# Biases off the matrix engine, quantised values transposed as 16-bit floats, and query and key rows restacked in 8 KB runs: a fused two-layer kernel on one core

## The chip, the cores and the metric

The kernel runs on one core of a Trainium2 chip. The metric is the device time of the whole program in microseconds, from the core's first to its last instruction as the runtime reports it; three runs of the kernel before gave 1095.13, 1095.16 and 1095.32 us (median 1095.16). A core has five engines with instruction streams of their own: PE (the 128x128 matrix engine), DVE (vector), ACT (scalar and activation), POOL (a second, slower vector engine) and SP, which here issues the DMA transfers. They meet only through semaphores.

## The reference

32 independent batches of 128 tokens with 256 features. With LN(v) = (v - mean) / sqrt(var + 1e-5), and mha() an attention of 16 heads of 16 features:

```
h  = LN(x)
a  = LN(h + mha(q=h, kv=h,   s_* weights and biases, mask S)) * ln1_g + ln1_b
c  = LN(a + mha(q=a, kv=ctx, c_* weights and biases, mask X)) * ln2_g + ln2_b
f  = relu(c @ ff_w1 + ff_b1) @ ff_w2 + ff_b2                 # 256 -> 1024 -> 256
x1 = x + tanh(g_x) * (LN(c + f) * ln3_g + ln3_b)
quant(v): s = 127 / max|v| per row, round(v * s) / s         # weights quantised to -1, 0, 1
g, u = quant(LN(x1)) @ w_gate.T, quant(LN(x1)) @ w_up.T      # 256 -> 1024
out  = x1 + tanh(g_f) * (quant(silu(g) * u) @ w_down.T)
```

## The kernel before

**Tiles.** A group is two batches (`G = 2`, `T = 256` tokens); there are 16 groups. A group passes through four stages: A (self attention), B (cross attention), C (the first feed-forward net) and E (the quantised one). The kernel is software-pipelined: iteration t works on stage A of group t-1, its preparation `Ap` of group t, B of group t-2, C of t-3 and E of t-4. So there are 20 iterations, the 5 first and 4 last written out and 11 in a hardware loop; iterations 4 to 15 have every stage at work.

**The order of the work** is a table, `SCHEDULE`, that all five engines walk in the same order, each doing its own part of a step. `("smax", k, quad)` and `("scores", k, half)` are the two score products of attention unit k (units 0 and 1 are the two batches of A, 2 and 3 those of B; 4 or -1 are the neighbours' in the next or last iteration); `values` the product with V; `R` turns its result back; `O` and `W` turn and project the output; `N` normalises; `M` turns the row maxima. `Ap` and `Bp` steps make the projections, `("in", s, t)` brings a stacked tensor back, `C F` and `C F2` are the two layers of the first net, `E GU`, `Q2` and `DN` gate/up, the second quantisation and the down projection. `BANK_OF` says which of four PSUM banks (lin_A, lin_B, lin_C, lin_E) a step writes. A step waits until its bank is read out and its inputs are there; an engine that waits holds up all that stands behind it.

**Precision by parts.** A 32-bit factor is split into an f16 high part and an f16 rest; `products` adds three products of parts.

**Biases.** They lie in two rows (high and rest) of `brows`. `bias` opens an accumulation with one matmul of `brows` against ones: two per projection of Q or K, two per `C F` step (line 595), one per `W` and per `C F2` (line 597).

**Quantised values.** ACT adds `MAGIC` = 1.5 * 2^23, which rounds to whole numbers in f32; PE turns the f32 tiles (`TQ` line 623, four blocks; `DN` line 760, four blocks for each of four steps), and ACT takes `MAGIC` off on the way out of PSUM (lines 859, 905).

**Restacking.** Scores need, for each head, its 16 rows of q (or k) high and rest stacked in the partitions. `parts_out` (line 472) writes both parts to DRAM as (2, 256 features, 256 tokens); `parts_in` (line 481) reads them back in four transfers of 16 partitions each, in runs of 512 bytes (one feature's 256 tokens). SP also copies the residuals `hres_A`, `hres_B` from `h` (lines 514, 507).

**Normalisation.** DVE takes the statistics (1067 to 1076), POOL the power -1/2 (1290), DVE applies it (1081), POOL multiplies by the gain (1308) and adds the bias (1316).

## Time and profile before

| | |
|---|---|
| median of 3 runs | 1095.16 us |
| profiled execution | 1097.78 us, span 1096.0 us |
| mean granted PE clock | 0.95 of full; 1.00 from 239 to 955 us |
| PE / DVE / ACT / POOL busy | 934.2 / 768.7 / 476.8 / 282.7 us |
| DMA | 85.02 MB in 136284 packets, 131631 of them under 2 KB |
| chain that ended last | PE 37%, DVE 24%, issue 14%, DMA 12%, POOL 5%, SP queue 5%, ACT 3% |

The profile is one execution. Busy time counts an engine's instructions; for PE, spans of consecutive matmuls overlap, so the distance between two starts is what a matmul costs the stream, and the printed mean is longer. "Idle before" is time in which an engine had no instruction running just before the rows of a group, with what ended it. The chain of waits follows the last instruction back through what released it each time.

### The profile page before, as it was taken

The page shows a single profiled execution, that of the slowest core. Times are in us where ns is not written, and L with a number is a line of the kernel's source. Part 1 is how long each engine was busy: PE and PEld are TensorE (multiplying, and loading weights), DVE is VectorE, ACT ScalarE, POOL GpSimd, SP SyncE. Part 2 cuts the span into 40 slices and gives each one's busy share as a digit, 9 for nine tenths or more (in the row PEclk, how much of TensorE's full clock was granted, in tenths as well). Part 3 has the DMA queues.
Part 4 walks back from the last instruction along what each step waited for, and adds up shares of the span by engine and source line. Part 5 has one row for each costly group of instructions (what it writes and reads, how often), then busy time and mean ns, then how long its engine had stood idle before and what let it go on. Part 6 is the DMA issues. An engine that isn't in the chain of part 4 may idle for free.

```text
span 1096.0 us, 26005 instructions
## 1 busy us (share of the span) xinstructions
PE 934.2 (85%) x8995; PEld 722.5 (66%) x8995; DVE 768.7 (70%) x1903; ACT 476.8 (44%) x769; POOL 282.7 (26%) x340
## 2 busy tenths in 40 slices
PE   1345869999999999999999999999999999877655
PEld 0224547768787777777777878687868687756442
DVE  7735555576878787877777787878787877664633
ACT  1113325254545455464545454545454545442422
POOL 7001112141323231323232323223141413140310
PEclk9959869999999999999999999999999999998885
DMA  6257273728191909081826464554637281514000
GB/s 166 89 85 133 63 86 74 93 63 104 44 133 40 135 29 144 29 137 37 127 47 111 53 101 72 84 75 88 83 80 91 65 99 49 60 49 39 21 10 10
DMA packets 136284, 85.02 MB, mean 78 GB/s; under 512 B 10632, under 2 KB 131631, under 8 KB 136240
## 3 DMA queue, kind: packets, MB, share of 16 engines
q1 hardware_dynamic: 136240, 84.43, 46.9%
q8 instruction: 28, 0.46, 0.2%
q14 instruction: 16, 0.13, 0.1%
HBM read 54.49 MB, written 20.98 MB: 69 GB/s over the span
## 4 chain that ended last, share of the span: by engine, by line
PE 37%; DVE 24%; issue 14%; DMA 12%; POOL 5%; SPq 5%; ACT 3%; DVEq 1%; POOLq 0%; ACTq 0%
DMA stk_BQ<-parts_BQ 9%; PE lin_C L747 5%; PE smax L663 4%; SPq L481 3%; PE lin_E L587 3%; PE lin_C L587 3%; POOL lrs L1290 3%; DVE nm_A L1145 2%; PE st L689 2%; DVE late L1081 2%; DVE lst L1067 2%; PE lin_E L736 2%; DVE am L1209 2%; PE lin_A L736 2%; PE lin_A L587 2%
## 5 line engine op out<-in xcount | busy, mean ns | idle before, releaser
L1290 POOL TENSOR_TENSOR lrs<-lve,neghalf 128x2 f32<-128x2 f32 (+1 forms) x112 | 71.0, 633 | 546.4 <-DVE lve L1076 546.3
L913 ACT ACTIVATE e<-st 128x1024 f32<-128x1024 f32 x128 | 130.8, 1022 | 58.8 <-PE st L689 57.9
L1145 DVE TENSOR_REDUCE nm_B<-smax 128x4 f32<-128x512 f32 x128 | 88.0, 687 | 55.0 <-PE smax L663 54.8
L1145 DVE TENSOR_REDUCE nm_A<-smax 128x4 f32<-128x512 f32 x128 | 87.9, 687 | 42.6 <-PE smax L663 39.3
L659 PE MATMUL smax<-mb,ident_big 128*128 128x512 f16 x128 | 52.6, 411 | 33.0 <-DVE nm_A L1145 23.0
L663 PE MATMUL smax<-stk_BK,stk_BQ 126*128 126x128 f16 x512 | 52.2, 226 | 19.3 <-DMA stk_BQ<-parts_BQ 14.5
L894 ACT ACTIVATE late<-late,magic_col,s 128x1024 f32<-128x1024 f32 x32 | 39.7, 1242 | 63.2 <-DVE s L1215 63.2
L919 ACT ACTIVATE av_sb<-av 128x512 f32<-128x512 f32 x64 | 37.9, 593 | 56.6 <-PE av L703 56.0
L663 PEld LDWEIGHTS smax<-stk_BK,stk_BQ 126*128 126x128 f16 x512 | 36.9, 100 | 33.3 <-DMA stk_BQ<-parts_BQ 11.5
L747 PE MATMUL lin_C<-w,late 128*128 128x256 f32 x256 | 57.9, 379 | 0.0
L747 PE MATMUL lin_A<-w,late 128*128 128x256 f32 x256 | 57.9, 379 | 0.0
L902 ACT ACTIVATE late<-lin_B,hcg 128x512 f32<-128x512 f32 x32 | 21.9, 686 | 81.8 <-PE lin_B L754 81.8
L663 PEld LDWEIGHTS smax<-stk_AK,stk_AQ 126*128 126x128 f16 x512 | 42.2, 103 | 17.5 <-issue 4.1
L663 PE MATMUL smax<-stk_AK,stk_AQ 126*128 126x128 f16 x512 | 53.2, 229 | 0.0
L684 PE MATMUL st<-mbT,ident_big 128*128 128x512 f16 x128 | 49.2, 384 | 3.6 <-ACT e L913 3.3
L747 PEld LDWEIGHTS lin_A<-w,late 128*128 128x128 f32 x256 | 47.4, 190 | 5.9
L747 PEld LDWEIGHTS lin_C<-w,late 128*128 128x128 f32 x256 | 47.4, 190 | 5.8
L689 PEld LDWEIGHTS st<-stk_AQ,stk_AK 128*128 128x128 f16 x512 | 39.7, 99 | 17.2 <-issue 0.6
L689 PE MATMUL st<-stk_AQ,stk_AK 128*128 128x128 f16 x512 | 50.0, 220 | 0.0
L659 PEld LDWEIGHTS smax<-mb,ident_big 128*128 128x128 f16 x128 | 12.6, 98 | 48.5 <-DVE nm_A L1145 33.0
L1296 POOL TENSOR_TENSOR qk_AQ<-qf_A,qk_AQ 128x512 f16<-128x512 f32 x16 | 18.5, 1157 | 97.9 <-ACT qk_AQ L867 97.9
L1081 DVE TENSOR_SCALAR late<-late,lmv,lrs 128x256 f32<-128x256 f32 x64 | 31.6, 535 | 15.3 <-POOL lrs L1290 15.2
(271 smaller groups left out, 2460.4 us busy)
## 6 DMA issues: line engine op xcount, KB each, us to landing
stk_AK<-parts_AK SPq DMA_DIRECT2D x64, 128.0 KB, 4.6
stk_AQ<-parts_AQ SPq DMA_DIRECT2D x64, 128.0 KB, 7.1
stk_BK<-parts_BK SPq DMA_DIRECT2D x64, 128.0 KB, 5.4
stk_BQ<-parts_BQ SPq DMA_DIRECT2D x64, 128.0 KB, 7.8
x_a<-in_x_dram SPq DMA_DIRECT2D x16, 256.0 KB, 2.9
cx<-in_ctx_dram SPq DMA_DIRECT2D x16, 256.0 KB, 2.8
parts_AK<-qk_AK SPq DMA_DIRECT2D x16, 256.0 KB, 6.4
parts_AQ<-qk_AQ SPq DMA_DIRECT2D x16, 256.0 KB, 4.5
```

What stands on the lines that cost most here:

```text
L587: mm = eng.matmul(dst, lhs(a, k), rhs(b, k), start=(start and at == 0), stop=(at == last))
L659: eng.matmul(smax[:, :], ident_big[:, :], mb[:, :].unsqueeze(1).to_broadcast([P, 4, P]), start=True, stop=True)
L663: mm = eng.matmul(smax[:, i * P:(i + 1) * P], stk[s, "Q"][0:XROW, h, tok], stk[s, "K"][0:XROW, h, tok], start=(s == "B"), stop=True, skip_ ...
L684: eng.matmul(st[:, k2 * 512:(k2 + 1) * 512], ident_big[:, :], mbT[:, :].unsqueeze(1).to_broadcast([P, 4, P]), start=True, stop=True)
L689: mm = eng.matmul(st[:, col:col + P], stk[s, "K"][:, h, tok], stk[s, "Q"][:, h, tok], start=(s == "B"), stop=True, skip_group_check=True)
L736: mm = eng.matmul(bank[:, 0:D], oT[s][:, c, :], wo[s][:, c, :], start=False, stop=(c == DC - 1))
L747: mm = eng.matmul(bank[:, 0:D], fT[:, c, k * P:(k + 1) * P], w2[:, c, :], start=False, stop=(c == FC - 1))
L894: eng.activation(q2m[:, :], z2[:, :], ACT.Identity, scale=s2[:, 0:1], bias=magic_col[:, 0:1]).then_inc(q2_ready, 1)
L913: eng.activation(e32[:, hf, :], st[:, :], ACT.Exp, scale=SCORE).then_inc(st_drained, 1)
L1081: i_ = eng.tensor_scalar(dst(k), src(k), lmv[n][:, k, 0:1], lrs[n][:, k:k + 1], ALU.subtract, ALU.mult)
L1145: eng.tensor_reduce(nm[s][:, 4 * part:4 * part + 4], smax[:, :].rearrange("p (h k) -> p h k", h=4), AX_X, ALU.max, negate=True).then_inc(s ...
L1290: eng.tensor_tensor(lrs[n][:, a:b], lve[n][:, a:b], neghalf[:, 0:b - a], ALU.pow).then_inc(ln_rstd[n], 1)
```

## The change

- The biases `s_bo`, `c_bo`, `ff_b2` are no longer matmuls in each `W` and `F2`. Three matmuls at the start spread them over the partitions, DVE makes `boA`, `lnbo_B` and `lnbo_C` (the latter two with `ln1_b`, `ln2_b` added), and POOL adds them into the residuals: `hres_A` and `hres_B` (128x512 each, in `residual`, in the place of SP's two copies) and a new `hres_C` (128x256 per batch, after `N`). `ff_b1` becomes the bias operand of the relu on ACT, which is one instruction per 256 columns in place of one per 512. The biases of Q and K stay on PE.
- ACT adds `MAGICQ` = MAGIC + 0x6600; the low 16 bits of the sum are then the f16 number 1536 + q. PE turns these halves (every second 16-bit element, f16 identity, f16 in PSUM), and ACT takes 1536 off.
- The columns of the Q and K weights are reordered within each half (by_dim, at the setup), so that 8 heads of one feature stand in 8 neighbouring partitions, and a partition's 2 x 256 columns are 1 KB. DRAM then holds, for one feature, 8 KB in one run. `parts_in` is two transfers of 32 partitions with 8 KB each. `parts_out` of a Q writes its high part twice, in a second transfer. `head_at` gives the head that stands in a slot.
- `SCHEDULE` and `BANK_OF` are new tables.

The core of the diff (the setup of reordered weights and bias rows, semaphore counts and the rest of the tables left out):

```diff
+LOW16 = 1536.0
+MAGICQ = MAGIC + 0x6600
...
+def head_at(slot):
+    return slot % DC * HB + slot // DC
...
-BIASES = [("s_bq", D), ("s_bk", D), ("c_bq", D), ("c_bk", D), ("ff_b1", F), ("s_bo", D), ("c_bo", D), ("ff_b2", D)]
+BIASES = [("s_bq", D), ("s_bk", D), ("c_bq", D), ("c_bk", D), ("s_bo", D), ("c_bo", D), ("ff_b2", D)]
...
-        part_dram = {(s, t): nc.dram_tensor(f"parts_{s}{t}", (2, D, T), F16).ap() for s in "AB" for t in "QK"}
+        part_dram = {(s, t): nc.dram_tensor(f"parts_{s}{t}", (3 if t == "Q" else 2, P, DC * T), F16).ap()
+                     for s in "AB" for t in "QK"}
...
-                eng.dma_start(part_dram[s, t].rearrange("q (c p) n -> p (q c) n", p=P),
-                              qk_parts[s, t][:, :, :]).then_inc(part_out[s, t], 16)
+                both = qk_parts[s, t][:, :, :].rearrange("p (q c) n -> p q (c n)", q=2)
+                eng.dma_start(part_dram[s, t][0:2].rearrange("q p x -> p q x"), both).then_inc(part_out[s, t], 16)
+                if t == "Q":
+                    eng.dma_start(part_dram[s, t][2], both[:, 0, :]).then_inc(part_out[s, t], 16)
 
             def parts_in(st_, s, t):
 
                 g = st_.g[s + "p"]
-                eng.wait_ge(part_out[s, t], g.at(16, 16))
-                for j in range(4):
-                    q = j // 2 if t == "Q" else j % 2
-                    eng.dma_start(stk[s, t][DH * j:DH * (j + 1), :, :],
-                                  part_dram[s, t][q].rearrange("(h d) n -> d h n", d=DH)).then_inc(stk_in[s, t], 16)
+                eng.wait_ge(part_out[s, t], g.at(PART_OUT[t], PART_OUT[t]))
+                for j in range(2):
+                    q = j if t == "Q" else 0
+                    rows = part_dram[s, t][q:q + 2].rearrange("q (d h) x -> (q d) (h x)", d=DH)
+                    eng.dma_start(stk[s, t][2 * DH * j:2 * DH * (j + 1), :, :].rearrange("p h n -> p (h n)"),
+                                  rows).then_inc(stk_in[s, t], 16)
...
-                        wait(eng, *st_.unit_read("W", -1))
-                        eng.dma_start(hres["B"][:, :, :], hin["B"][:, :, :]).then_inc(hres_in["B"], 16)
...
-                        wait(eng, *st_.unit_read("W", 1))
-                        eng.dma_start(hres["A"][:, :, :], hin["A"][:, :, :]).then_inc(hres_in["A"], 16)
...
-                            mm = eng.transpose(bank[:, at:at + P], q1m[:, b, c * P:(c + 1) * P], ident[:, :])
+                            low = q1m[:, b, c * P:(c + 1) * P].bitcast(F16).rearrange("p (n two) -> p n two", two=2)
+                            mm = eng.transpose(bank[:, :].bitcast(F16)[:, at:at + P], low[:, :, 0], ident16[:, :])
...
-                        bias(dst, "ff_b1", f * P, P, T)
...
-                for i in range(8):
-                    h = 8 * hf + i
+                for i in (0, 2, 4, 6, 1, 3, 5, 7):
+                    h = head_at(8 * hf + i)
...
-                bias(bank[:, 0:D], "s_bo" if s == "A" else "c_bo", 0, D, 0)
...
-                    bias(bank[:, 0:D], "ff_b2", 0, D, 0)
...
+            for i, name in enumerate(("s_bo", "c_bo", "ff_b2")):
+                col = BCOL[name]
+                eng.matmul(st[:, i * D:(i + 1) * D], ones16[:, 0:P], brows[:, col:col + D], start=True,
+                           stop=True).then_inc(u_pe, 1)
             first = first_steps()
-            for st_ in first[0:3]:
+            iteration(first[0])
+            eng.wait_ge(u_bo, 3)
...
-                    f, func = 2 * name[1], ACT.Relu
-                    eng.activation(fT[:, f:f + 2, :].rearrange("p f n -> p (f n)"), src, func).then_inc(drain, 1)
+                    for j in range(2):
+                        f = 2 * name[1] + j
+                        a_ = eng.activation(fT[:, f, :], bank[:, j * T:(j + 1) * T], ACT.Relu, bias=b1w[:, f:f + 1])
+                    a_.then_inc(drain, 1)
...
-                    eng.wait_ge(ln_bias[2], g.at(G, k + 1))
-                    eng.scalar_tensor_tensor(res["C"][:, k, :], bank[:, 0:D], 1.0 / (WS * WS), hin["C"][:, k, :],
+                    eng.wait_ge(hres_in["C"], g.at(G, k + 1))
+                    eng.scalar_tensor_tensor(res["C"][:, k, :], bank[:, 0:D], 1.0 / (WS * WS), hres["C"][:, k, :],
                                              ALU.mult, ALU.add).then_inc(drain, 1)
...
+            n_bo = [0]
+            eng.wait_ge(u_pe, 8)
+            setup(eng.tensor_scalar(boA[:, :], st[:, 0:D], 1.0 / WS, None, ALU.mult), u_bo, n_bo)
+            setup(eng.scalar_tensor_tensor(lnbo["B"][:, :], st[:, D:2 * D], 1.0 / WS, lnb[1][:, :], ALU.mult, ALU.add), u_bo, n_bo)
+            setup(eng.scalar_tensor_tensor(lnbo["C"][:, :], st[:, 2 * D:3 * D], 1.0 / (WS * WS), lnb[2][:, :], ALU.mult,
+                                           ALU.add), u_bo, n_bo)
...
+                    if s == "B":
+                        eng.tensor_tensor(hres["C"][:, b, :], tg[s][:, b, :], lnbo["C"][:, :], ALU.add).then_inc(hres_in["C"], 1)
+            def residual(st_, s):
+                if st_.reg is None and st_.t == 0:
+                    eng.wait_ge(u_bo, 3)
+                if s == "A":
+                    eng.wait_ge(ln_out[0], st_.g["Ap"].at(1, 1))
+                    wait(eng, *st_.unit_read("W", 1))
+                    src, add = hin["A"], boA
+                else:
+                    eng.wait_ge(ln_gain[1], st_.g["Bp"].at(G, G))
+                    wait(eng, *st_.unit_read("W", -1))
+                    src, add = tg["A"], lnbo["B"]
+                eng.tensor_tensor(hres[s][:, :, :], src[:, :, :], add[:, :].unsqueeze(1).to_broadcast([P, G, D]),
+                                  ALU.add).then_inc(hres_in[s], 1)
...
+                    elif step == ("Ap", "V"):
+                        residual(st_, "A")
+                    elif step == ("Bp", "Q"):
+                        residual(st_, "B")
```

PE around the first net's four `F` steps and the second layer. Before, rows of one iteration (`L595` and `L597` are biases, `L587` the products of the first layer, `L747` of the second, `L663` smax of B, `L736` the output projection):

```order
L663 MATMUL smax<-stk_BK,stk_BQ 128x128 x4
L595 MATMUL lin_C<-ones,brows 128x256
L587 MATMUL lin_C<-hT_C,w_0 128x256 x2
L587 MATMUL lin_C<-hT_C,w_1 128x256
L587 MATMUL lin_C<-hT_C,w_0 128x256 x2
L587 MATMUL lin_C<-hT_C,w_1 128x256
L595 MATMUL lin_C<-ones,brows 128x256
```

Now, the same step (`L610` the products, `L683` smax of B) and what follows it:

```order
L683 MATMUL smax<-stk_BK,stk_BQ 128x128 x4
L772 MATMUL lin_A<-wuT,q1T 128x512 x2
L755 MATMUL lin_E<-wo_A,oT_A 128x256 x2
L772 MATMUL lin_B<-wgT,q1T 128x512 x2
L693 MATMUL lin_C<-ident,nm_B 32x128
L683 MATMUL smax<-stk_BK,stk_BQ 128x128 x4
L772 MATMUL lin_E<-wuT,q1T 128x512 x2
L765 MATMUL lin_A<-w,late 128x256 x8
```

No `brows` row stands ahead of the projections (L755) or of the second layer (L765), and the gate and up products (L772) of the second batch now lie before the second layer instead of after it.

SP from the query rows of B to the read-back of A. Before:

```order
L472 DMA parts_BQ<-qk_BQ 128x4x256
L507 DMA hres_B<-h 128x512
L481 DMA stk_BK<-parts_BK 16x16x256 x4
L481 DMA stk_BQ<-parts_BQ 16x16x256 x4
L472 DMA parts_AK<-qk_AK 128x4x256
L519 DMA x_c<-in_x_dram 128x2x256
L472 DMA parts_AQ<-qk_AQ 128x4x256
```

Now:

```order
L499 DMA parts_BQ<-qk_BQ 128x2x512
L501 DMA parts_BQ<-qk_BQ 128x512
L510 DMA stk_BK<-parts_BK 32x4096 x2
L510 DMA stk_BQ<-parts_BQ 32x4096 x2
L542 DMA x_c<-in_x_dram 128x2x256
L499 DMA parts_AK<-qk_AK 128x2x512
L499 DMA parts_AQ<-qk_AQ 128x2x512
```

The residual copy is gone, a second write of the query rows has come, and eight reads are four.

DVE around the second layer of the first net and the second quantisation (`L1184`, now `L1226`, is the residual sum after `F2`; `L1209`, now `L1251`, the maximum of the second quantisation; `L1200` and `L1205`, now `L1242` and `L1247`, the gate and up products). Before:

```order
L1184 SCALAR_TENSOR_TENSOR late<-lin_C,h 128x256
L1142 REGISTER_ALU
L1145 TENSOR_REDUCE nm_B<-smax 128x4
L1199 REGISTER_ALU
L1200 SCALAR_TENSOR_TENSOR late<-late,lin_B 128x512
L1202 REGISTER_ALU
L1203 REGISTER_ALU
L1205 TENSOR_TENSOR late<-late,lin_E 128x512
L1209 TENSOR_REDUCE am<-late 128x1
```

Now:

```order
L1247 TENSOR_TENSOR late<-late,lin_E 128x512
L1224 REGISTER_ALU
L1226 SCALAR_TENSOR_TENSOR late<-lin_A,hres_C 128x256
L1184 REGISTER_ALU
L1187 TENSOR_REDUCE nm_B<-smax 128x4
L78 REGISTER_ALU
L1123 TENSOR_SCALAR nrm_A<-res_A,lmv,lrs 128x256
L1251 TENSOR_REDUCE am<-late 128x1
```

The gate and up products have moved ahead of the first `F2`; the maximum still follows it.

## Rows read from the trace of the kernel before

**Rows 1.** The page, busy us (share of the span) xinstructions

```profile
PE 934.2 (85%) x8995; PEld 722.5 (66%) x8995; DVE 768.7 (70%) x1903; ACT 476.8 (44%) x769; POOL 282.7 (26%) x340
```

**Rows 2.** Windows: start:end, length, busy us (x) of PE, PEld, DVE, ACT, POOL; clock, DMA

```profile
0.00:186.00 186.00, 101.12 (x873) 71.77 (x877) 110.53 (x202) 48.31 (x73) 38.77 (x44) 0.83 0.48 96
...
515.00:570.00 55.00, 53.10 (x531) 42.47 (x532) 43.30 (x110) 27.30 (x44) 15.84 (x19) 1.00 0.55 87
```

**Rows 3.** Timeline of ACT, line 859, first and thirteenth of 16: start, us

```profile
239.58 0.60 ACT L859 ACTIVATE q1T<-lin_A 128x512 bf16<-128x512 f32 x1
...
926.77 0.60 ACT L859 ACTIVATE q1T<-lin_A 128x512 bf16<-128x512 f32 x1
```

**Rows 4.** Waits of PE, 460 to 1010 us: total us, times, longest

```profile
PE smax L659 <- DVE nm_A L1145: 11.1, 17, 1.0
PE smax L663 <- DMA stk_BQ<-parts_BQ: 8.9, 7, 3.9
```

**Rows 5.** Timeline of PE: start, us of the group

```profile
522.26 0.39 PE L663 MATMUL smax<-stk_AK,stk_AQ 126*128 126x128 f16 x4
522.49 0.60 PE L617 MATMUL lin_C<-ident,h 128*128 128x128 f32 x4
522.93 0.38 PE L684 MATMUL st<-mbT,ident_big 128*128 128x512 f16 x1
...
551.00 0.28 PE L597 MATMUL lin_C<-brows,ones 128*128 128x256 f16 x1
551.11 3.62 PE L747 MATMUL lin_C<-w,late 128*128 128x256 f32 x16
554.56 0.39 PE L663 MATMUL smax<-stk_BK,stk_BQ 126*128 126x128 f16 x4
```

**Rows 6.** Groups by shape, ACT: busy us, mean ns, idle before

```profile
L852 ACT ACTIVATE late<-late,magic_col,s 128x256 f32<-128x256 f32 x32 | 17.5, 594 | 49.1 <-DVE kap L1110 49.1
...
L928 ACT ACTIVATE oT_B<-lin_E 128x256 f32<-128x256 f32 x32 | 12.4, 388 | 31.2 <-PE lin_E L724 31.2
...
L883 ACT ACTIVATE late<-lin_C 128x512 f32<-128x512 f32 x16 | 9.6, 597 | 18.5 <-PE lin_C L587 18.5
```

**Rows 7.** The page, DMA issues: KB each, us to landing

```profile
stk_BQ<-parts_BQ SPq DMA_DIRECT2D x64, 128.0 KB, 7.8
x_a<-in_x_dram SPq DMA_DIRECT2D x16, 256.0 KB, 2.9
...
parts_AQ<-qk_AQ SPq DMA_DIRECT2D x16, 256.0 KB, 4.5
```

**Rows 8.** Chain of waits, steady and first iterations: start, us, what

```profile
101.88 7.99 DMA stk_AQ<-parts_AQ
...
190.99 7.86 DMA stk_BQ<-parts_BQ
...
533.85 8.78 DMA stk_BQ<-parts_BQ
```

**Rows 9.** Timeline of POOL: start, us

```profile
509.70 1.27 POOL L1328 TENSOR_TENSOR late<-late,lnb 128x512 f32<-128x512 f32 x1
511.13 1.31 POOL L1333 TENSOR_TENSOR late<-late,x_c 128x512 f32<-128x512 f32 x1 [0.16 <-POOL late L1328]
...
515.78 0.73 POOL L1316 TENSOR_TENSOR h<-tg_B,lnb 128x256 f32<-128x256 f32 x1 [0.16 <-POOL tg_B L1308]
```

**Rows 10.** Timeline of DVE, same columns

```profile
491.68 0.17 DVE L1154 SCALAR_TENSOR_TENSOR nm_B<-nm_B 128x16 f16<-128x16 f32 x1
...
500.26 1.22 DVE L1209 TENSOR_REDUCE am<-late 128x1 f32<-128x1024 f32 x1
...
511.34 1.13 DVE L1154 SCALAR_TENSOR_TENSOR nm_A<-nm_A 128x16 f16<-128x16 f32 x1
```

**Rows 11.** Timelines at an iteration's start, DVE, then PE

```profile
515.00 0.69 DVE L1145 TENSOR_REDUCE nm_A<-smax 128x4 f32<-128x512 f32 x1 [0.18 <-issue]
...
515.75 0.39 PE L659 MATMUL smax<-mb,ident_big 128*128 128x512 f16 x1 [0.92 <-DVE nm_A L1145]
```

More of the change, by code:

```diff
@@ L589, in products, with bias @@
                 return mm
-            def bias(dst, name, start_col, width, tokens):
+            def bias(dst, name, start_col, tokens):
                 col = BCOL[name] + start_col
-                if tokens:
-                    eng.matmul(dst, brows[:, col:col + P], ones16[:, 0:tokens], start=True, stop=False)
-                else:
-                    eng.matmul(dst, ones16[:, 0:P], brows[:, col:col + width], start=True, stop=False)
+                eng.matmul(dst, brows[:, col:col + P], ones16[:, 0:tokens], start=True, stop=False)
             def prep(st_, s, name):
@@ L858, in prep @@
                     eng.wait_ge(fill, after)
-                    eng.activation(q1T[:, :, :].rearrange("p c n -> p (c n)"), bank[:, :], ACT.Copy,
-                                   bias=-MAGIC).then_inc(drain, 1)
+                    eng.activation(q1T[:, :, :].rearrange("p c n -> p (c n)"), bank[:, :].bitcast(F16)[:, 0:DC * T], ACT.Copy,
+                                   bias=-LOW16).then_inc(drain, 1)
                     return
@@ L893, in beside @@
                         wait(eng, *st_.full("E", ("DN", k - 1, 1)))
[L894 removed]
+                    eng.activation(q2m[:, :], z2[:, :], ACT.Identity, scale=s2[:, 0:1], bias=magicq[:, 0:1]).then_inc(q2_ready, 1)
                     return
@@ L1005, in low_part @@
                 eng.wait_ge(u_hi, sum(1 for m in range(n + 1) if m not in WHOLE))
+                if n in BY_DIM:
+                    for x_ in range(DC * DC):
+                        i_ = eng.scalar_tensor_tensor(by_dim(lo)[:, x_, :, :], heads_of(raw[n])[:, x_, :, :], WS,
+                                                      by_dim(hi)[:, x_, :, :], ALU.mult, ALU.subtract)
+                    setup(i_, u_lo, n_lo)
+                    return
                 setup(eng.scalar_tensor_tensor(lo[:, :, :].rearrange("p c n -> p (c n)"), raw[n], WS,
@@ L1244, in _ @@
             first = first_steps()
-            for st_ in first[0:3]:
-                iteration(st_)
-            for st_ in first[3:]:
+            iteration(first[0])
+            n_bo = [0]
[4 more added lines that the diff above has]
+                                           ALU.add), u_bo, n_bo)
+            for st_ in first[1:]:
                 iteration(st_)
@@ L1311, in unit_step @@
                         wait(eng, *st_.full("B", "T"))
-                        wait(eng, hres_in["B"], g.back(1).at(16, 16))
                     else:
```

80 lines of the change are left out of this document (56 added, 24 removed), and 38 rows, old and new, of tables (BANK_OF, SCHEDULE).

## The prediction

> **What bounds the kernel now.** I read four views, from coarse to fine. The page first: PE is busy 85% of the span, DVE 70%, ACT 44%, POOL 26% [rows 1]. Then the windows: of 55 us in mid-kernel PE is busy 53.1 and DVE 43.3, of the first 186 us PE only 101; its granted clock is 1.00 of full (2.4 GHz) in the one and 0.83 on the mean in the other [rows 2]. So the kernel has two regimes: a steady one in which PE is nearly full, and two ends that live on latency. The steady one is measured by one instruction that comes once an iteration: the turned quantised values leave PSUM at 239.58 us and, twelve iterations on, at 926.77 [rows 3]. That is (926.77 - 239.58) / 12 = 57.27 us an iteration, 687 us of the 1096. What stops PE there: in 550 us (9.6 iterations) it waits 11.1 us for DVE's row maxima and 8.9 us for the stacked query rows of stage B [rows 4], 1.16 and 0.93 us an iteration; the other waits are small. The chain of waits tells the less comfortable half: it does not stay on PE. In one steady iteration it goes through a transfer of 8.78 us (query rows of B), and in the ramp through transfers of 7.99 and 7.86 us [rows 8]. PE is full, but DVE, POOL and DMA chains end only just in time beside it.
>
> **Biases off PE.** A bias matmul costs the stream the distance between its start and the next: 551.11 - 551.00 = 0.11 us [rows 5]. In an iteration 8 go from `F`, 4 from `W`, 2 from `F2`: 14 x 0.11 = 1.54 us.
>
> **Transposes in f16.** Four f32 blocks take 522.93 - 522.49 = 0.44 us; four f16 products of 128 columns take 522.49 - 522.26 = 0.23 us [rows 5]. Twenty blocks an iteration (4 `TQ`, 16 `DN`) change from one to the other: 5 x 0.21 = 1.05 us. The trace has no f16 transpose with a stride of two in its weights. The bounds are 0 (it costs as the f32 one) and 1.05; I take 1.05, since the nearest row by type and columns is the f16 one.
>
> The Trainium skill's "TensorE: Matmul & The Clock Gate", the part on sustained rate, gives about 81 ns per matmul of 128 columns. By it four blocks would cost 0.32 us, and the term would be 0.58 us instead of 1.05. The trace has 0.23 us for four, 57 ns each, so I go by the trace.
>
> PE sheds 1.54 + 1.05 = 2.59 us of 57.27 an iteration.
>
> **Restacking.** A tensor of 512 KB now comes by four transfers of 128 KB, landing 7.8 us after issue by the median, in runs of 512 bytes; x comes with 256 KB in runs of 1 KB in 2.9 us [rows 7]. The changed read is two such 256 KB transfers in runs of 8 KB. Its bounds are 2.9 us and the old 7.8; I take 4.5, nearer to the row of x, since two follow each other. Against it: a query tensor is written with 384 KB instead of 256, where 256 KB landed in 4.5 us [rows 7], which I take as 1 us more, and SP waits for both. Net some 2.5 us sooner, and SP has four transfers fewer ahead of the B query read and no residual copy. In the steady state this can give no more than the wait it ends, 0.93 us; I take 0.9. The new order puts four `smax` of B between `F` steps, about the same distance behind `Bp Q`, so the wait should not come back.
>
> **Residuals on POOL.** POOL gets two sums of 128x512, 1.27 us each, and two of 128x256, 0.73 us each [rows 9]: 2.54 + 1.46 = 4.0 us an iteration on an engine busy 15.8 of 55 [rows 2]. The `residual` of B stands ahead of the power for unit -1: POOL waits for DVE's sum of `W -1`, then holds 1.27 us, beside which DVE takes the statistics of that unit. That makes DVE's `N -1` late by less than 1.27 us, I take 0.4; behind it are `GU` and a scores step, so PE is hidden. The `residual` of A stands behind the power of `W 2` and ahead of `N 2`. Its 1.27 us delay the gain and bias of B's last unit and then the power of E's norm; I count 1 us of room there. I cost all this at 0.1 us.
>
> A more direct cost is seen in the trace: the 16-column rest of the maxima takes DVE 0.17 us at 491.68, and 1.13 us at 511.34, ending at 512.47, as POOL's sum of 511.13 + 1.31 = 512.44 ends [rows 9, 10]. So a POOL sum can hold a small DVE step for its whole length. Four more sums an iteration are four more chances. If each hit costs 0.5 us and half of them hit, DVE loses 1 us, of which PE sees some 0.3.
>
> The Trainium skill's "SBUF — State Buffer", section "Who interferes with whom", says that these two share one port pair as an exclusive lock, and the loser blocks until the other is through; by that rule, the trace agrees.
>
> **Relu.** One instruction of 128x512 at 0.597 us becomes two of 128x256, each between 0.388 (no operand for the bias) and 0.594 us (with one) [rows 6]. Eight an iteration: 3.1 to 4.8 us against 2.4, on an engine that is half idle. The `F` rows come 0.2 to 0.6 us later; only the last before `F2` matters, and gate and projection steps lie between them now. Cost: 0.
>
> **The order.** At an iteration's start DVE is behind: the first maxima are taken at 515.00, and PE's second `smax` waits 0.92 us for them [rows 11]. The table changes nothing in the first ten steps, so a stall of this kind stays, and as PE comes sooner by what it sheds in the tail it may grow by 0.2 us. What gets better is the stretch from `F2 0` on: the gate and up products of the second batch are done before it, so that the quantisation's maximum, 1.22 us on DVE [rows 10], no longer waits for them. I take 0.3 us of gain, between -1 and +1.5.
>
> **The sum.** An iteration: 2.59 (PE) + 0.9 (transfer) - 0.1 (residuals) - 0.3 (held DVE steps) - 0.2 (start) + 0.3 (order) = 3.2 us, times 12 = 38 us. The ends hold four groups' worth of the same PE work, 4 x 2.59 = 10.4 us, in a regime where PE is busy half the time: 5 us. In the ramp four reads lie open at about 8 us (two of them shown [rows 8]); at 2.5 us less each they give 10, of which I keep 7, since other waits are next. The setup gains by shorter bias rows and loses by weights split in four pieces, three more matmuls and a wait: 0. Sum 38 + 5 + 7 = 50 us. The profiled execution, 1097.8 us, would become 1048; it lies 2.6 us over the median, which becomes 1095.2 - 50 = 1045 us.
>
> **Rivals.**
> 1. *The chain holds, not PE.* The chain of waits leaves PE for DVE, POOL and the transfer in much of a steady iteration. What PE sheds there turns into waiting, above all for the maxima. For it: 1.16 us of that wait are there already. Against it: DVE has 11.7 us free of 55. If half of PE's gain goes, an iteration gives 1.3 + 0.5 = 1.8, so 22 us, and with 8 from the ends 30: 1065 us.
> 2. *The strided weights cost as much as before.* Then 1.05 x 16 = 17 us are missing: 1045 + 17 = 1062 us.
> 3. *The order is better than I can see.* PE is idle 1.9 of 55 us [rows 2], 2.0 an iteration, of which my sum takes away 0.6 net. If all goes, that is 12 x 1.4 = 17 us more: 1028 us. For it: PE is the fullest engine by 10 us. Against it: the waits for maxima at the iteration's start, where the order is the old one.
> 4. *Slower: POOL holds DVE.* Each of the four new sums blocks a DVE step in full, and the late norms stop PE: 4.0 us more waiting against 2.59 less work, 1.4 us an iteration, 17 us in twelve, with nothing from the ends: 1112 us. It decides from 2.6 us of new waits an iteration on; 2.0 us are idle now. For it speaks the step held for 1.13 us [rows 10], against it that DVE is idle 11.7 of 55 us and that few such steps are there.
> 5. *The reads are no faster.* 32 runs of 8 KB could serve the 16 engines worse than 256 of 512 bytes; then 0.9 x 12 + 7 = 18 us are missing: 1063 us.
>
> **Numbers.** Forecast 0.5; rivals 1, 2 and 5 together 0.27; rival 3 0.12; rival 4 0.06; near zero, gains and waits in balance, 0.05. A measurement of this kernel can tell about 0.2%, 2.2 us. Faster by more 0.89, within 0.04, slower 0.07. The range runs from rival 3 to a little past rival 1: 1026 to 1070 us.
>
> **What the profile would show.** PE work: no `brows` rows but for Q and K, four turned blocks in 0.23 us, an iteration of 54 us between two `q1T`. Reads: a `stk_BQ` landing at 4 to 5 us, no wait of PE for it, and prologue transfers of that length in the chain. POOL: 20 us busy in 55, and few DVE steps of 16 columns beyond 0.2 us. I am wrong in mechanism if the iteration is over 55.5 us, if the waits for `nm_A` or `nm_B` exceed 2 us an iteration, or if `lin` rows of `TQ` keep a distance of 0.11 us.

## The result, and the profile after

The changed kernel takes 1057.64 us, the median of four runs (1056.64 to 1058.59), against 1095.14 for the kernel before on the same chip: a ratio of 0.966, with a 95% interval of 0.9643 to 0.9676. Forecast were 1045 us and a range of 1026 to 1070. So the sign and the range hold, and 12.6 us of the forecast gain did not come. The profiled execution of after has a span of 1054.9 us, 41.1 less than that of before; the working below goes by this pair.

The page of after, its busy line (us, share of the span, instructions), then its DMA packets and one line of the DMA issues (KB each, us to landing):

```profile
PE 891.9 (85%) x8730; PEld 687.2 (65%) x8774; DVE 780.6 (74%) x1921; ACT 501.2 (48%) x833; POOL 343.3 (33%) x405
...
DMA packets 57450, 80.81 MB, mean 77 GB/s; under 512 B 9623, under 2 KB 52798, under 8 KB 53310
...
stk_BQ<-parts_BQ SPq DMA_DIRECT2D x32, 256.0 KB, 5.0
```

Against [rows 1] PE is busy 42.3 us less in the whole span and POOL 60.6 us more. Some 7 of the 42.3 us are no saving: this trace lacks 44 matmul records (8730 beside 8774 weight loads). The trace of x2 below, with the same matmuls and all 8774 records, has PE busy 899.2 us. Against [rows 7] the query rows of B land after 5.0 us instead of 7.8, and packets fell from 136284 to 57450.

The windows of [rows 2], now (start:end, length, busy us and count of PE, PEld, DVE, ACT, POOL; granted clock, DMA share, GB/s):

```profile
0.00:186.00 186.00, 99.47 (x857) 70.18 (x858) 122.90 (x219) 54.36 (x73) 45.30 (x50) 0.86 0.32 93
515.00:570.00 55.00, 52.56 (x542) 41.48 (x544) 44.31 (x116) 29.94 (x51) 19.97 (x25) 1.00 0.32 80
```

The second row says that the steady state is what it was: PE nearly full at its full clock. POOL's 19.97 us is the 20 that was forecast. The first shows DVE 12 us busier in the ramp, most of it by the setup, below: with another setup (x2) DVE is busy 771.6 us in the whole span instead of 780.6.

The instruction that came once an iteration at 239.58 and 926.77 [rows 3] is now on line 887. Its first and thirteenth start in after are 235.00 and 896.90 us, so an iteration takes (896.90 - 235.00) / 12 = 55.16 us instead of 57.27. The 41.1 us are then 25.3 from twelve iterations, 4.6 before the first of them and 11.2 after the thirteenth start (158.0 us against 169.2).

The waits of PE in after, 294 to 900 us, 11.0 iterations (total us, times, longest):

```profile
PE smax L679 <- DVE nm_A L1187: 20.1, 22, 1.4
PE lin_E L693 <- DVE nm_A L1196: 2.8, 11, 0.3
PE lin_A L772 <- issue: 1.8, 11, 0.2
PE smax L683 <- DMA stk_BQ<-parts_BQ: 0.9, 3, 0.3
```

and in before over the same window, 10.6 iterations:

```profile
PE smax L659 <- DVE nm_A L1145: 13.3, 20, 1.0
PE smax L663 <- DMA stk_BQ<-parts_BQ: 4.2, 6, 1.3
PE smax L659 <- issue: 0.5, 2, 0.3
PE lin_A L595 <- DVE late L1200: 0.2, 1, 0.2
```

That makes 18.2 / 10.58 = 1.72 us an iteration before and 25.6 / 10.99 = 2.33 after. What is left of an iteration, PE's own stream with its small gaps, is 55.55 and 52.83. One row of after is no wait: `lin_A L772 <- issue` stands where the record of a matmul is missing (three of the sixteen matmuls of `L772` in an iteration; x2, with all its records, has no such row). Without it the waits are 2.16 and the rest is 52.99. So PE shed 2.6 to 2.7 us, as forecast (2.59), and the waits grew by 0.45 to 0.61 where the forecast had them shrink by 0.6. That difference is the size of the whole miss of the steady state. It does not say yet what the order of the steps has to do with it; x6 does. The transfer's wait is gone (0.40 to 0.08), the wait for stage A's maxima grew from 1.26 to 1.83, and a new one (line 693) is 0.25.

**Where the new wait comes from.** DVE in after, at the start of an iteration (start, us):

```profile
553.67 1.27 DVE L1123 TENSOR_SCALAR nrm_B<-res_B,lmv,lrs 128x256 f32<-128x256 f32 x1 [0.73 <-POOL lrs L1338]
554.87 0.68 DVE L1187 TENSOR_REDUCE nm_A<-smax 128x4 f32<-128x512 f32 x1
```

POOL in after, the same stretch:

```profile
553.02 0.55 POOL L1338 TENSOR_TENSOR lrs<-lve,neghalf 128x1 f32<-128x1 f32 x1 [1.63 <-DVE lve L1118]
553.53 1.26 POOL L1384 TENSOR_TENSOR hres_A<-h,boA 128x512 f32<-128x512 f32 x1
```

PE in after:

```profile
555.61 0.39 PE L679 MATMUL smax<-mb,ident_big 128*128 128x512 f16 x1 [1.43 <-DVE nm_A L1187]
```

Read them together. POOL delivers the power and at once starts the new residual sum of A, which ends at 554.79. DVE's normalising step starts beside it and is through only at 554.94, after 1.27 us. Behind that step on DVE stands the maximum for which PE waits: 1.43 us, where it was 0.92 [rows 11]. Over the whole run the step takes 793 ns on the mean (groups of DVE in after, busy us and mean ns):

```profile
L1123 DVE TENSOR_SCALAR nrm_B<-res_B,lmv,lrs 128x256 f32<-128x256 f32 x32 | 25.4, 793 | 19.0 <-POOL lrs L1338 19.0
...
L1194 DVE TENSOR_SCALAR nm_A<-nm_A 128x16 f16<-128x16 f32 x32 | 19.0, 595 | 3.2
...
L1196 DVE SCALAR_TENSOR_TENSOR nm_A<-nm_A 128x16 f16<-128x16 f32 x32 | 5.6, 175 | 1.1
```

In before these are:

```profile
L1081 DVE TENSOR_SCALAR nrm_B<-res_B,lmv,lrs 128x256 f32<-128x256 f32 x32 | 13.1, 409 | 11.8 <-POOL lrs L1290 11.7
...
L1152 DVE TENSOR_SCALAR nm_A<-nm_A 128x16 f16<-128x16 f32 x32 | 17.1, 536 | 3.2
L1154 DVE SCALAR_TENSOR_TENSOR nm_A<-nm_A 128x16 f16<-128x16 f32 x32 | 13.2, 413 | 1.1
```

The held step of [rows 10] (the rest of the maxima, 1.13 us) is gone, 413 to 175 ns, and a step that PE waits for is held instead. The two have different causes. Groups of DVE in x7, the kernel before with nothing but the new order:

```profile
L1081 DVE TENSOR_SCALAR nrm_B<-res_B,lmv,lrs 128x256 f32<-128x256 f32 x32 | 13.2, 413 | 13.1 <-POOL lrs L1290 12.4
...
L1154 DVE SCALAR_TENSOR_TENSOR nm_A<-nm_A 128x16 f16<-128x16 f32 x32 | 5.6, 175 | 1.1
```

The order alone frees the small step; the new sum holds `nrm_B`. The Trainium skill ("SBUF — State Buffer", "Who interferes with whom") has the two engines block each other for a whole instruction on a shared port pair. The trace agrees in the main: the held step ends 0.15 us after the sum. But it takes 0.41 us when alone, so one that could do nothing before the sum's end should end 0.41 us after it; these rows don't settle why it ends sooner.

**The setup.** DVE in after:

```profile
25.45 2.43 DVE L1038 SCALAR_TENSOR_TENSOR w_AQ<-late,w_AQ 128x128 f16<-128x128 f32 x4
...
40.08 2.42 DVE L1061 CAST e<-late 1x1024 f16<-1x1024 f32 x1
```

The same piece in before:

```profile
25.85 0.69 DVE L1006 SCALAR_TENSOR_TENSOR w_AQ<-late,w_AQ 128x512 f16<-128x512 f32 x1
```

The reordered weights are written as f16 with 16 bytes from one element to the next: 2.43 us for four quarters instead of 0.69 for the whole. The bias rows are cast in the same manner, and leave for their place late. SP in after:

```profile
48.80 0.65 SPq L483 DMA_DIRECT2D brows<-e  x1
```

and in before:

```profile
38.60 0.65 SPq L457 DMA_DIRECT2D brows<-e  x1
```

That is 10.2 us later for what every projection of Q and K needs. I had costed the setup at 0.

### The profile page after: what moved, and what is told of

The parts are those of the page before. It is cut to its first block, busy times and chain, and to the rows that moved or that the text cites. A ratio compares the mean times of both kernels' runs of the same rounds, so it can differ in the third digit from the quotient of the medians.

```text
span 1054.9 us, 25741 instructions
## 1 busy us (share of the span) xinstructions
PE 891.9 (85%) x8730; PEld 687.2 (65%) x8774; DVE 780.6 (74%) x1921; ACT 501.2 (48%) x833; POOL 343.3 (33%) x405
## 4 chain that ended last, share of the span: by engine, by line
PE 49%; DVE 16%; issue 13%; POOL 11%; DMA 7%; ACT 2%; SPq 1%; POOLq 0%; DVEq 0%; ACTq 0%
PE lin_A L765 11%; PE lin_B L610 5%; PE lin_C L610 4%; PE smax L683 4%; PE lin_E L610 4%; DMA stk_BQ<-parts_BQ 3%; PE st L709 3%; PE av L723 3%; POOL lrs L1338 2%; PE lin_C L755 2%; POOL late L1402 2%; DVE late L1123 2%; POOL late L1397 2%; POOL late L1394 2%; PE lin_C L783 2%
## 5 line engine op out<-in xcount | busy, mean ns | idle before, releaser
L765 PE MATMUL lin_A<-w,late 128*128 128x256 f32 x512 | 116.8, 381 | 0.1
L765 PEld LDWEIGHTS lin_A<-w,late 128*128 128x128 f32 x512 | 95.8, 190 | 14.3 <-DVE late L1247 0.4
L683 PE MATMUL smax<-stk_BK,stk_BQ 126*128 126x128 f16 x512 | 52.0, 226 | 11.4 <-DMA stk_BQ<-parts_BQ 7.5
L683 PEld LDWEIGHTS smax<-stk_BK,stk_BQ 126*128 126x128 f16 x512 | 36.7, 100 | 23.8 <-DVE nm_B L1187 7.8
L683 PEld LDWEIGHTS smax<-stk_AK,stk_AQ 126*128 126x128 f16 x512 | 41.2, 100 | 16.9 <-issue 2.7
L683 PE MATMUL smax<-stk_AK,stk_AQ 126*128 126x128 f16 x512 | 51.9, 225 | 0.0
L1360 POOL TENSOR_TENSOR tg_A<-nrm_A,lng 128x256 f32<-128x256 f32 x32 | 23.2, 725 | 83.2 <-DVE nrm_A L1123 73.1
L610 PE MATMUL lin_C<-hT_C,w 128*128 128x256 f16 x384 | 48.9, 279 | 0.7 <-DVE hT_C L1164 0.7
L924 ACT ACTIVATE late<-late,magicq,s 128x1024 f32<-128x1024 f32 x32 | 39.7, 1241 | 18.5 <-DVE s L1257 18.5
L1344 POOL TENSOR_TENSOR qk_BK<-qf_B,qk_BK 128x512 f16<-128x512 f32 x16 | 18.5, 1159 | 78.6 <-ACT qk_BK L895 74.5
L723 PE MATMUL av<-e,v_A 128*32 128x128 f32 x1024 | 41.2, 278 | 2.8 <-ACT e L943 2.8
```

The lines of the kernel that those rows point to most:

```text
L610: mm = eng.matmul(dst, lhs(a, k), rhs(b, k), start=(start and at == 0), stop=(at == last))
L683: mm = eng.matmul(smax[:, i * P:(i + 1) * P], stk[s, "Q"][0:XROW, h, tok], stk[s, "K"][0:XROW, h, tok], start=(s == "B"), stop=True, skip_ ...
L723: mm = eng.matmul(av[VA * j:VA * (j + 1), c * P:(c + 1) * P], v32[s][:, b, h, :], e32[:, hf, i * P:(i + 1) * P], start=True, stop=True)
L765: mm = eng.matmul(bank[:, 0:D], fT[:, c, k * P:(k + 1) * P], w2[:, c, :], start=(c == 0), stop=(c == FC - 1))
L924: eng.activation(q2m[:, :], z2[:, :], ACT.Identity, scale=s2[:, 0:1], bias=magicq[:, 0:1]).then_inc(q2_ready, 1)
```

## The experiments

Each kernel is the changed one with the edit shown, unless said otherwise. They ran on three chips: x1 to x4 on one, where the kernel before took 1095.74 us, x5 to x8 on the second (1096.10), x9 to x11 on the third (1097.81). The changed kernel was measured in one session only, beside 1095.14. The ratio column takes this into account, a difference of medians doesn't, so the gains in us below are good to 3 or 4 us. By the ratios x1, x2, x5, x10 and x11 lie 8, 10, 16, 9 and 26 us under the changed kernel, each to 3 or 4 us. An iteration is read from one profiled execution of each kernel. In the table an iteration is a twelfth of the distance between first and thirteenth `q1T`; waits are all that the view of PE's waits lists for 294 to 900 us, by the iterations in it; rest is the difference. The view leaves out waits under 0.15 us and shows a missing record as a wait of 0.16 us an iteration, so waits and rest are good to about 0.2 us: x2, whose steady state is that of after, shows how much.

| kernel | median us | ratio to before, 95% | iteration | waits | rest | first q1T |
|---|---|---|---|---|---|---|
| before | 1095.14 | 1 | 57.27 | 1.72 | 55.55 | 239.58 |
| after | 1057.64 | 0.966 (0.9643 to 0.9676) | 55.16 | 2.33 | 52.83 | 235.00 |
| x1 | 1049.98 | 0.9587 (0.9556 to 0.9619) | 54.59 | 1.60 | 52.99 | 236.62 |
| x2 | 1049.93 | 0.9573 (0.9543 to 0.9602) | 55.14 | 2.17 | 52.97 | 228.12 |
| x3 | 1072.36 | 0.9766 (0.9728 to 0.9803) | 56.05 | 1.82 | 54.23 | 237.85 |
| x4 | 1067.45 | 0.9739 (0.9707 to 0.9772) | 55.80 | 2.11 | 53.69 | 236.36 |
| x5 | 1043.11 | 0.9518 (0.9493 to 0.9544) | 54.54 | 1.84 | 52.70 | 228.42 |
| x6 | 1081.44 | 0.9862 (0.9833 to 0.989) | 56.60 | 3.12 | 53.48 | 238.95 |
| x7 | 1156.99 | 1.0549 (1.0518 to 1.0581) | 61.56 | 5.04 | 56.52 | 243.75 |
| x8 | 1116.41 | 1.0184 (1.0143 to 1.0226) | 58.64 | 4.97 | 53.67 | 241.59 |
| x9 | 1084.88 | 0.9879 (0.9844 to 0.9914) | 56.75 | 3.36 | 53.39 | 239.88 |
| x10 | 1051.20 | 0.9576 (0.9542 to 0.961) | 54.66 | 1.70 | 52.96 | 236.32 |
| x11 | 1034.53 | 0.9422 (0.9396 to 0.9448) | 53.93 | 1.09 | 52.84 | 228.78 |

**x1: the residual sum of A moved.** POOL does it between the bias and the residual of stage C's output, some 5 us earlier; where C is not active it stays.

```diff
+                    if active("Ap", st_.t):
+                        residual(st_, "A")
...
-                        residual(st_, "A")
+                        if not active("C", st_.t):
+                            residual(st_, "A")
```

> The changed kernel with one POOL sum moved: hres_A is made inside the step C apply, between the bias and the x1 sum, where POOL is idle for 1.14 to 1.24 us, instead of at Ap V. Theory A (the held DVE step): in the changed kernel nrm_B takes 0.79 us on the mean instead of 0.41, because hres_A runs beside it, and PE stands 1.43 us at the second smax of each iteration. Without it nrm_B returns to 0.41, the wait to about 0.6, the iteration from 55.16 to 54.3 us, the whole to 1043 to 1048 us. Rival B (the wait is set by another chain, POOL's x1 and power): nrm_B gets short, but the iteration stays within 0.2 us of 55.16 and the time at 1055 to 1058.

DVE in x1, the step again and the maximum behind it:

```profile
553.41 0.41 DVE L1123 TENSOR_SCALAR nrm_B<-res_B,lmv,lrs 128x256 f32<-128x256 f32 x1 [0.74 <-POOL lrs L1338]
554.00 0.69 DVE L1187 TENSOR_REDUCE nm_A<-smax 128x4 f32<-128x512 f32 x1 [0.18 <-issue]
```

1.27 us is 0.41 again, and the wait for A's maxima in 294 to 900 us fell from 20.1 to 13.4 us. That is 0.57 us an iteration and 7.7 us of the median, with no instruction added or taken away. It confirms that the sum held the step, and that PE paid for it, though less than theory A had it: 54.59 us an iteration and not 54.3, 1049.98 us and not 1043 to 1048. The wait for the maxima is 0.9 us at the longest, where 0.6 was expected.

**x2: the reordered weights written contiguously.** The pieces are walked in the order of the destination, and the large steps fall on the f32 reads.

```diff
-            return tile[:, :, :].rearrange("p c (m d h) -> p (c m) h d", m=DC, d=DH)
+            return tile[:, :, :].rearrange("p c (m d h) -> p (c m) d h", m=DC, d=DH)
...
-            return flat.rearrange("p (x h d) -> p x h d", h=HB, d=DH)
+            return flat.rearrange("p (x h d) -> p x d h", h=HB, d=DH)
...
```

> The changed kernel with the reordering of weights and bias rows in the setup walked the other way: the inner index is the head, so that the f16 output is written contiguously and the f32 input is read with a step of 64 bytes. Theory A: what made the split weights slow (2.43 us a matrix on DVE instead of 0.69, 2.47 on ACT instead of 0.63; bias rows 2.42 and 4.68 us) is the write of single 2-byte elements 16 bytes apart; with contiguous writes each DVE piece falls from 0.6 to 0.25 us and the setup ends 8 to 10 us sooner, time 1047 to 1051. Rival B: a strided read costs the same as the strided write; no change, 1056 to 1059.

DVE in x2:

```profile
25.46 1.19 DVE L1038 SCALAR_TENSOR_TENSOR w_AQ<-late,w_AQ 128x128 f16<-128x128 f32 x4
...
35.12 1.01 DVE L1061 CAST e<-late 1x1024 f16<-1x1024 f32 x1
```

Half the time for the same values, and on ACT too (`w_AQ` 1.06 us instead of 2.47); the bias rows leave at 39.61 us, the first `q1T` comes 6.9 us sooner, the iteration is that of after, and the median falls by 7.7 us. The 6.9 is good to 2 or 3 us: x1, x3 and x4, with the setup of after, have their first `q1T` at 236.36 to 237.85 and not at 235.00.

**x3: the quantised values turned as f32 again.**

```diff
-                        mm = eng.transpose(bank[:, :].bitcast(F16)[:, f * P:(f + 1) * P], low[:, :, 0], ident16[:, :])
+                        mm = eng.transpose(bank[:, f * P:(f + 1) * P], q2m[:, at:at + P], ident[:, :])
```

> The changed kernel with the quantised values turned as f32 again (MAGIC, f32 identity, f32 in PSUM), all else as changed: 20 blocks an iteration at 0.11 instead of 0.055 us, 1.05 us of PE an iteration. Theory A (PE bounds the iteration, its waits are a fixed addition): iteration 56.1 us, time 1069 to 1074. Rival B (the chain over DVE and POOL holds): under 0.4 us an iteration, 1058 to 1063.

PE in x3 turns four blocks in 545.18 - 544.74 = 0.44 us:

```profile
544.74 0.61 PE L777 MATMUL lin_B<-ident,late 128*128 128x128 f32 x4
545.18 0.60 PE L777 MATMUL lin_E<-ident,late 128*128 128x128 f32 x4
```

and in after in 0.22:

```profile
537.01 0.39 PE L779 MATMUL lin_B<-ident,late 128*128 128x128 f16 x4
537.23 0.39 PE L779 MATMUL lin_E<-ident,late 128*128 128x128 f16 x4
```

So the f16 read with a stride of two costs no more than f16 products of 128 columns did [rows 5], and 1.05 us of PE work an iteration is worth 0.89 us of time, 14.7 us of the median (12 by the ratios).

**x4: PE work added.** One more matmul of 256 columns ahead of each half of an `F` step, as the biases had stood; its result is overwritten.

```diff
+                        eng.matmul(dst, brows[:, 0:P], ones16[:, 0:T], start=True, stop=True)
```

> The changed kernel with one 256-column f16 matmul more ahead of each half of an F step (the next product overwrites it): 8 x 0.11 = 0.88 us of PE an iteration, the work of the F biases that the change took out. Theory A (PE bounds): iteration 56.0 us, time 1067 to 1072. Rival B (PE has slack beside the chain): under 0.3 us an iteration, 1057 to 1062.

Eight of them, 0.88 us, cost 0.64 us an iteration and 9.8 us in all. With x3: 73 to 85% of PE work turns into time here, the rest is taken up by waits that shrink.

**x5: x1 and x2 together.**

> The moved hres_A and the setup with contiguous writes together, all else as changed. Theory A (two costs apart, one in the setup, one in each iteration): the gains add, 7.7 + 7.7 us under the changed kernel, 1041 to 1044 us. Rival B: they overlap, since the iteration or the ends lose again what the other gives; 1047 or more.

1043.11 us, 14.5 under after; apart they gave 7.7 and 7.7. The two add, one in the iterations (54.54), the other ahead of them (228.42). This is about the forecast's 1045.

**x6: the change with the old order.** `SCHEDULE` and `BANK_OF` are those of before.

```diff
-    ("setup", 1), ("smax", 2, 0), ("C", ("F", 0)), ("smax", 2, 1), ("C", ("F", 1)), ("E", "Q2", 0), ("smax", 2, 2),
...
+    ("values", 1, 1), ("R", 0), ("E", "GU", 1, 1), ("in", "A", "K"), ("C", ("F", 0)), ("C", ("F", 1)), ("O", 0),
```

> The changed kernel with SCHEDULE and BANK_OF of the kernel before. Theory A (the new order is what turns the shed PE work into time): with the old order the second quantisation holds DVE ahead of the maxima and more than 1 us an iteration is lost; iteration 56.0 to 56.5 us, time 1067 to 1075. Rival B (the work shed is what counts, the order is worth under 0.3 us): 1055 to 1061.

The new order is worth 1.44 us an iteration and 23.8 us in all, not 0.3 and some 4, and more than theory A had. Put the other way: in the old order all the rest of the change brings only 57.27 - 56.60 = 0.67 us an iteration, though PE sheds its 2.6 there too. The largest waits of PE in x6:

```profile
PE smax L679 <- DVE nm_A L1187: 21.5, 31, 1.6
PE lin_C L617 <- DVE hT_B L1164: 4.2, 11, 0.4
PE lin_E L744 <- DVE o_B L1205: 3.0, 10, 0.3
PE lin_E L744 <- DVE late L1247: 2.0, 11, 0.2
```

It stands at more places for DVE. The listed waits explain 0.8 of the 1.44. The rest, 0.65, is in longer distances between matmuls. A little of it is the clock: after a wait of 1.92 us at 907.69 it is at half once in the twelve iterations (0.72 on the mean from 906 to 912 us), which makes 0.14 us each. What makes the rest is open.

**x7: the old kernel with the new order.** Only the two tables change in the kernel before.

> The kernel before with SCHEDULE and BANK_OF of the change, nothing else. Theory A (the order is worth 0.5 us or more by itself): iteration 56.5 to 56.8 us, 1086 to 1091 us. Rival B (it is laid out for the cheaper steps and the shorter reads, and without them the transfer of B's query rows comes late): PE waits for stk_BQ over 1 us an iteration, 1095 to 1110 us.

5.5% slower than before. The wait of PE that leads its list:

```profile
PE smax L663 <- DMA stk_BQ<-parts_BQ: 35.6, 10, 4.7
```

The transfer that cost 0.40 us an iteration costs 3.6. Rival B had the direction, at over 1 us an iteration and 1095 to 1110 us; the loss is several times that. The order by itself is bad; it needs reads that land early.

**x8: the restacking undone.** Heads, rows and the four reads of before, in the new order.

```diff
-                for j in range(2):
-                    q = j if t == "Q" else 0
-                    rows = part_dram[s, t][q:q + 2].rearrange("q (d h) x -> (q d) (h x)", d=DH)
...
+                for j in range(4):
+                    q = j // 2 if t == "Q" else j % 2
...
```

> The changed kernel with the restacking undone: DRAM by features, four reads of 16 partitions in runs of 512 bytes, one write, weights and bias rows in their own order. Theory A (the short reads matter in the ramp and at B's smax in the new order): the setup gives 10 us back, but PE waits 1 to 2 us an iteration for stk_BQ and the open reads of the ramp are 3 us longer each; 1060 to 1075 us. Rival B (the reads were hidden in the steady state): iteration 55.2 us as in the changed kernel, and only setup and ramp differ, in balance; 1052 to 1058 us.

3.48 us an iteration worse than after, and 1.8% slower than before; both theories had expected far less (1052 to 1075 us). The wait of PE that leads the list of x8:

```profile
PE smax L680 <- DMA stk_BQ<-parts_BQ: 28.2, 10, 3.8
```

The waits make 2.64 of the 3.48. The rest, 0.84, is seen behind some of these waits. PE in x8, at one of them and at another of the same length:

```profile
546.95 0.54 PE L680 MATMUL smax<-stk_BK,stk_BQ 126*128 126x128 f16 x4 [2.85 <-DMA stk_BQ<-parts_BQ]
547.28 2.77 PE L607 MATMUL lin_C<-hT_C,w 128*128 128x256 f16 x12
549.84 0.63 PE L680 MATMUL smax<-stk_BK,stk_BQ 126*128 126x128 f16 x4
...
432.05 0.40 PE L680 MATMUL smax<-stk_BK,stk_BQ 126*128 126x128 f16 x4 [2.94 <-DMA stk_BQ<-parts_BQ]
432.30 1.47 PE L607 MATMUL lin_C<-hT_C,w 128*128 128x256 f16 x12
433.61 0.39 PE L680 MATMUL smax<-stk_BK,stk_BQ 126*128 126x128 f16 x4
```

and the windows of x8 from 1 us before PE's return to 5 us behind it (granted clock is the third number from the end):

```profile
431.05:437.05 6.00, 5.00 (x52) 4.60 (x52) 3.61 (x8) 2.15 (x5) 0.54 (x1) 1.00 0.95 186
...
545.95:551.95 6.00, 5.00 (x37) 4.03 (x38) 2.13 (x3) 0.91 (x3) 0.63 (x1) 0.72 0.98 184
```

After the wait of 2.85 us twelve matmuls take 2.56 us instead of 1.31, at half the clock, and the window loses (1 - 0.72) x 6.00 = 1.7 us of PE's work. After the one of 2.94 us nothing of the kind happens: 1.31 us, clock 1.00. The same window around each of the twelve waits between first and thirteenth `q1T` has 0.72 six times and 1.00 six times, and the length does not decide: 0.72 behind waits of 2.27 and 2.51 us, 1.00 behind 2.72, 2.88 and 2.94. Six times 1.7 us in twelve iterations are 0.85 us each, the size of the rest. So a late transfer is paid once as the wait, and in half of the cases here a second time in matmuls at half the clock.

**x9: x6 with the sum moved as in x1.**

> The changed kernel with the old SCHEDULE and BANK_OF, and hres_A moved on POOL to between the bias and the x1 sum. With the old order and hres_A in its place an iteration takes 56.60 us, and nrm_B is held as with the new one (0.79 us on the mean). Theory A (the held step is one fixed part of the stall at an iteration's start, in either order): iteration 56.0 us, time 1072 to 1076. Rival B (in the old order DVE is behind anyway, by the second quantisation, and POOL has no gap in C apply): 56.4 to 56.8 us, 1079 to 1084.

Nothing gained: 56.75 against 56.60 us an iteration, a ratio of 0.9879 against 0.9862. Groups of DVE in x9:

```profile
L1194 DVE TENSOR_SCALAR nm_A<-nm_A 128x16 f16<-128x16 f32 x32 | 24.9, 777 | 3.2
L1196 DVE SCALAR_TENSOR_TENSOR nm_A<-nm_A 128x16 f16<-128x16 f32 x32 | 18.8, 586 | 1.1
L1123 DVE TENSOR_SCALAR nrm_B<-res_B,lmv,lrs 128x256 f32<-128x256 f32 x32 | 14.1, 439 | 12.8 <-POOL lrs L1338 12.8
```

`nrm_B` is free (439 ns), but the small steps of A's maxima are held in its stead (777 and 586 ns). A sum on POOL has no price of its own; its place beside DVE's steps has.

**x10: one maximum moved.** The first `smax` of unit 1 goes from the start of an iteration to before the last `N` of the one before.

```diff
-    ("smax", 1, 0), ("Bp", "X"), ("values", -1, 0), ("smax", 1, 1), ("values", -1, 1), ("scores", 0, 0),
+    ("Bp", "X"), ("values", -1, 0), ("smax", 1, 1), ("values", -1, 1), ("scores", 0, 0),
...
-    ("smax", 4, 2), ("O", 2), ("E", "DN", 1, 2), ("smax", 4, 3), ("W", 2), ("scores", 3, 1), ("Ap", "V"), ("N", 2),
-    ("M", 4),
+    ("smax", 4, 2), ("O", 2), ("E", "DN", 1, 2), ("smax", 4, 3), ("W", 2), ("scores", 3, 1), ("Ap", "V"), ("smax", 5, 0),
+    ("N", 2), ("M", 4),
```

> The changed kernel with the first smax of an iteration taken out of its start and put ahead of the last N step of the iteration before (the same product and maximum, for unit 5). DVE then takes that maximum while it waits 0.73 us for POOL's power, and not behind nrm_B. Theory A (the 1.43 us stall at the second smax is DVE's queue, held nrm_B and all): the stall all but goes, iteration 55.16 to 53.9 us, time 1040 to 1045. Rival B (the next link of DVE's chain, the statistics of E's norm ahead of the third smax, is late by as much): iteration 54.8 to 55.2, 1053 to 1058.

0.5 us an iteration, 6.4 us in all. The first stall is gone, but one of the next `smax` waits. PE in x10:

```profile
507.38 0.39 PE L679 MATMUL smax<-mb,ident_big 128*128 128x512 f16 x1 [1.04 <-DVE nm_A L1187]
```

In 294 to 900 us the waits for A's maxima went from 22 to 11 and from 20.1 to 10.8 us, that for the query rows of B from 0.9 to 3.2. The result lies between the two theories, an iteration nearer to rival B (54.8) than to theory A (53.9).

**x11: x1, x2 and x10 together.**

> The changed kernel with all three: hres_A moved, contiguous writes in the setup, first smax ahead. Theory A: the first smax ahead already hides most of what the held nrm_B cost, so this gives 7 to 8 us from the setup and 2 to 4 more from hres_A under the run with the first smax ahead alone; iteration 53.6 us, time 1031 to 1036. Rival B (the stall only moves on to the third and fourth smax): iteration 54.4 us, 1040 to 1043.

1034.53 us (1031.06 to 1036.70, six runs), a ratio of 0.9422: 23 us under the changed kernel and the fastest here. Waits of PE in x11:

```profile
PE smax L679 <- DVE nm_A L1187: 3.7, 11, 0.4
PE smax L683 <- DMA stk_BQ<-parts_BQ: 3.3, 5, 1.4
PE lin_E L693 <- DVE nm_A L1196: 2.7, 11, 0.3
```

Apart the three gave 7.7, 7.7 and 6.4 = 21.8 us, together 23.1; by the ratios 27 and 26. They add within the noise: neither the sum moved nor the maximum moved hides the other's gain.

## Why the prediction was right, and where it missed

- **PE's shed work** (2.59 us an iteration): right. The rest fell by 2.72, or 2.56 without the missing records; no bias row is left before the output projections and second layer, and four turned blocks take 0.22 us. Rival 2 is out (x3). That so much of it became time is another matter, and hangs on the order (below).
- **The transfer** (0.9): mis-sized. The reads are faster, 5.0 us where I took 4.5, and rival 5 is out. But the wait to be won was 0.40 us an iteration, not 0.93: the window of [rows 4] reached to 1010 us, beyond the steady state, and held a wait of 3.9 us of the tail. Measured gain 0.32. The window should have ended where the steady state does.
- **Residuals on POOL and held DVE steps** (-0.1 and -0.3): mechanism right, size and place wrong. I counted "1 us of room" for the residual of A and looked at who waits for POOL, not at who runs beside it. x1 prices that one sum at 0.57 us an iteration. It also takes up the growth at the iteration's start, for which I had 0.2: nm_A rose by 0.57 in all. The held 16-column step, on which I based the half hits, was relieved instead, by the order alone (175 ns in x7, 353 in x6).
- **The order** (+0.3): mis-sized, and wrongly treated as a term. With the change it is worth 1.44 us an iteration (x6), without it -4.3 (x7); restacking is worth 3.48 in the new order (x8). The two belong together: that the wait for the query rows "should not come back" in the new order was right only through the faster reads.
- **Luck in the total.** My sum without the order was 3.19 - 0.3 = 2.9 us an iteration; x6 measures 0.67 for it. The order, for which I had 0.3, gives 1.44. An error of -2.2 and one of +1.1 leave 1.1 short in 3.2. Had the order been worth its 0.3 and all else as measured, the time would be some 1057.6 + 12 x 1.14 = 1071 us (an estimate), just outside the range. That the range held is in part this cancelling.
- **The steady sum** (3.2): 2.11. Twelve times 1.08 is 13 us, the size of the whole miss.
- **The ends** (12 us with the setup at 0): 15.8. The tail gave 11.2; PE's busy time after the thirteenth start fell from 123.0 to 115.0 us. Ahead of the first `q1T` came 4.6, of which the setup had eaten 7 to 10: x2 gives 6.9 back there. The step "0" for the setup failed; it compared counts of instructions and not the stride with which they write. A larger gain at the ends covered the error in the sum, which is luck too. It comes mostly with the shorter reads, for which I had 7 us in the ramp and nothing in the tail. x8, with the old reads and a quick setup, has its first `q1T` at 241.59 us, x2 at 228.12; from the thirteenth to the end x8 takes 169.0 us (1114.3 - 945.3), where after takes 158.0 and x6, with the old order, 161.6.
- **Relu** (0): nothing against it. The instruction with a bias takes 470 ns, between the 388 and 594 of [rows 6].
- **Rival 1** (half of PE's gain lost): in the new order it is out: x3 and x4 give 0.85 and 0.73 of PE work back as time, not 0.5, and the waits grew through POOL's sum (x1). In the old order it is what happened, and more: 0.67 of the 2.6 us shed came through (x6), while PE waited at more places for DVE. **Rival 4**, POOL holding DVE, happened at a quarter of its price per iteration or less: 0.57 us of waiting from one sum, where it needed 2.6. **Rival 3** (1028 us) did not come true; x11 comes near its time, with more than the order changed.
- My own marks: iteration 55.16, under 55.5; waits for maxima 1.83 plus 0.25, just over the 2 us at which I had called the mechanism wrong. By that mark the mechanism of the waits was wrong, and one misplaced sum is enough to explain it (x1: 13.4 + 2.8 us in 11.1 iterations, 1.46). Few DVE steps of 16 columns should have been longer than 0.2 us: line 1194 takes 595 ns on the mean.

Open: what of the 1.44 us of the order lies outside the listed waits; whether a place exists for the sum of A in the old order; what decides whether the clock falls after a wait; and the 590 ns of `nm_A` (line 1194), which takes 175 when nothing holds it and in before, after, x1, x7, x9 and x11 ends 0.03 us after an instruction of POOL.
